# 304 of the 800 columns of a scatter of edges moved from five dense stages into two gather stages

## The chip, the cores and the metric

The kernel runs on one core of one Trainium2 chip. The metric is the device time of one launch in microseconds (us), a median over runs.

## The reference

A graph of 6250 nodes with 256 features and 100,000 edges (src, dst) goes through two layers. Cut to what matters here:

```
xn = layernorm(x)
# layer 0: two graph convolutions, each over all edges, then a linear attention and a linear layer
agg = segment_sum(relu(xn[src]), dst);   h = xn + agg;   out = relu(h @ w11 + b11) @ w12 + b12      # twice
x = x + relu(2 * out) + mix(xn);         x = x + layernorm(x) @ w.T + bias
# layer 1: attention over the same edges, but summed by src; a linear attention; a mixture of experts
e = exp(leaky_relu(el[src] + er[dst]));  w = e / segment_sum(e, src)[src];  out = segment_sum(w * x[dst], src)
```

Layer 0 sums by dst, the order in which the edges come. Layer 1 sums by src. So between the two the edges have to be put into the order of their sources.

## The kernel before

The program is a row of stages, each with its own semaphores and a barrier of all engines at its end; a stage ends with its slowest engine. Within one, every engine has its own instruction stream and they meet at semaphores. Nodes stand in 49 tiles of 128. The edges, packed into one int32 each (`m.packed`), stand as 125 lanes by 800 columns.

**Order by source.** `stage_count` counts the sources by tile. Inside the first convolution VectorE and TensorE then work out each edge's place: chunk c of 10 columns in round c (`Ranking.dve_read`, `dve_rank`, lines 789 to 796), 80 chunks, written over `m.key` as float32. At the end of that stage one VectorE cast makes `m.rank_i` of it (line 1058). After that the class `Scatter` (line 799 on) sends columns to DRAM (`m.edges[1]`): per column one indirect DMA on GpSimd's queue writes 125 single int32 values, each to its own place (line 818). It works in batches of 8: two small copies by GpSimd into staging tiles (lines 813, 814), a wait for them, 8 DMAs, and a wait for the batch two back. Five stages have it as GpSimd's only work, beside dense work on the other engines: mlp1 (144 columns), mlp2 (144), ffn (176), akv (176), aq (160). `stage_slots` reads the finished list before the attention over edges.

**A convolution** (`stage_conv`, conv1 and conv2) goes over 832 slots of 128 edges, 104 rounds of 8 (`RING`). GpSimd gathers 128 rows of 1 KB per slot (line 994), straight-line code without a loop; ahead of round r it waits until round r - 4 has been summed (its buffers) and until round r - 1 has landed:

```
for r in range(ROUNDS):
    if r >= DEEP: pool.wait_ge(summed, (r - DEEP + 1) * RING)
    if r >= 1:    pool.wait_ge(got[(r - 1) % DEEP], ...)      # round r - 1 has landed
    for k in range(RING): pool.indirect_dma_start(msg[...], None, table, ... m.GI[:, t:t + 1] ...)
```

ScalarE makes a one-hot of each slot's targets, TensorE multiplies it with the messages (line 1070), VectorE adds the product to the node's tile in `ACC` (line 1043). conv1 has the ranking beside it in rounds 0 to 79. conv2 has the keys' and values' sums of the linear attention beside it (`KeyValueSums`), with loads on SyncE's queue. The index lists of all gathers are the columns of `m.GI`, 896 wide.

After conv1 comes mlp1, then conv2, a short stage mix, mlp2, statistics, ffn, statistics, akv, aq, an addition, `stage_slots`, and the attention over edges.

Of the kernel before, what the change touches and what calls it, by code (L numbers as in the profile page):

```python
# [14 lines left out]
CH = 10  # L15
# [917 lines left out]

def stage_conv(nc, m, name, table, rank_sources, sum_keys):

# [1 line left out]
    with Stage(nc, name) as st:  # L941
# [5 lines left out]
        kv = KeyValueSums(nc, m, st) if sum_keys else None  # L947
        got = st.sems("got", DEEP)
        s_made, summed, added = st.sem("s_made"), st.sem("summed"), st.sem("added")
        tv, tt, ta = (st.sem(n) for n in ("turns_v", "turns_t", "turns_a"))  # L950
        ts = st.sem("turns_s")
        block = st.block()
        ROUNDS, CHUNKS = SLOT_TILES // RING, COLS // CH
# [23 lines left out]

        last_chunk = lambda r: isinstance(r, int) and r == CHUNKS - 1

        def landed(r, h):  # L980

            return (r - h) * (16 * RING // DEEP) + 16 * RING

        @block.gpsimd
        def _(pool):
            for r in range(ROUNDS):
                h = r % DEEP
                if r >= DEEP:
                    pool.wait_ge(summed, (r - DEEP + 1) * RING)
                if r >= 1:  # L990
                    pool.wait_ge(got[(r - 1) % DEEP], ((r - 1) // DEEP + 1) * 16 * RING)
                for k in range(RING):
                    t = r * RING + k
                    pool.indirect_dma_start(msg[:, h * RING + k, :], None, table,  # L994
                                            bass.IndirectOffsetOnAxis(ap=m.GI[:, t:t + 1], axis=0)).then_inc(got[h], 16)

        @block.scalar
        def _(act):
# [31 lines left out]
        def _(v):  # L1030
            def tile(r, h, chunk, keys):
                if chunk is not None:
                    ranking.dve_read(v, tv, r)
                    if not last_chunk(r):
                        ranking.dve_one_hot(v, tv, r + 1, 1 - h % 2)
                if keys is not None and h % 2 == 0 and not (isinstance(keys, int) and keys == 0):
                    kv.dve_norm(v, tv, keys - 1)
                starts = [v.snap(b * AW) for b in bins_of_round(nc, m, DVE, r)]
                for k in range(RING):
                    v.drain()  # L1040
                    v.wait_ge(summed, r * RING + k + 1)
                    acc = cols(m.ACC, starts[k], D)
                    nc.vector.tensor_tensor(acc, acc, ps[k % NB][:, 0:D], ALU.add).then_inc(added, 1)  # L1043
                if keys is not None and h % 2 == 1:
                    kv.dve_center(v, tv, keys)
                if chunk is not None:
                    ranking.dve_rank(v, r, h % 2)

            if sum_keys:
                nc.vector.memset(kv.vn[:, :, :], 1.0)  # L1050
# [3 lines left out]
            if sum_keys:  # L1054
                kv.dve_norm(v, tv, TILES - 1)
                kv.dve_end(v)
            if rank_sources:
                nc.vector.tensor_copy(m.rank_i[:, :], m.key[:, :])

        @block.tensor  # L1060
        def _(pe):
# [1381 lines left out]
def stages_before_attention(nc, m, dense):  # L2443
# [25 lines left out]
    stage_count(nc, m, 1)  # L2469
    stage_stats(nc, m, "stats0", 1e-5)  # L2470
    stage_norm(nc, m)
    stage_conv(nc, m, "conv1", m.relu_xn_table, True, False)

    stage_mlp(nc, m, "mlp1", m.w11s, m.b11s, m.w12s, m.b12r, False, (0, 144))
    stage_conv(nc, m, "conv2", m.conv1_table, False, True)
    m.wqkvs = sb("wqkvs", [P, 2, 3 * D])
    m.wouts = sb("wouts", [P, 2, D])
    m.boutr, m.mw2r = (sb(n, [P, D]) for n in ("boutr", "mw2r"))
    stage_mix(nc, m)
    stage_mlp(nc, m, "mlp2", m.w21s, m.b21s, m.w22s, m.b22r, True, (144, 144))  # L2480
    stage_stats(nc, m, "stats1", 1e-5)
    stage_ffn(nc, m, (288, 176))
    stage_stats(nc, m, "stats2", 1e-5, with_rms=True)
    stage_attn_kv(nc, m, (464, 176))
    stage_attn_q(nc, m, (640, 160))
    stage_attn_add(nc, m)
    stage_slots(nc, m, 1)

# [110 lines left out]
```

## Time and profile before

| | us |
|---|---|
| median of 3 runs (7104.03 to 7115.21) | 7106.12 |
| profiled execution, its own time | 7045.45 |
| its span, first to last instruction | 7043.1 |
| conv1: first gather to last addition | 358.6 to 1668.5 |
| mlp1 | 1669 to 1905 |
| conv2 | 1905 to 3215 |
| mlp2 | 3228 to 3466 |
| ffn | 3485 to 3772 |
| akv | 3794 to 4080 |
| aq | 4080 to 4343 |

Busy over the whole span: TensorE 49%, VectorE 40%, ScalarE 27%, GpSimd 51%. PE is TensorE's multiplications, PEld its loads of weights, DVE VectorE, ACT ScalarE, POOL GpSimd, SP SyncE. On GpSimd a DMA's duration is the time that the engine takes to issue it, not the transfer. A row of a timeline has start, duration, engine, line, operation, what is written and read, and in brackets the idle time before with what ended it; "issue" means that the trace names no releaser. A row of a table by stretches has the stretch, its length, then busy us with the count of instructions in brackets for PE, PEld, DVE, ACT and POOL, the granted clock of TensorE as a share of full speed, the mean busy share of the DMA engines and GB/s; where it is of one line, only that line's engine has a column.

### The profile page before, as it was taken

Reading aid. Unit: us, or ns where it says so; the run is one execution under the profiler, and the core shown is the slowest. Engines: PE = TensorE matmul, PEld = TensorE weight load, DVE = VectorE, ACT = ScalarE, POOL = GpSimd, SP = SyncE. Lnnn points to the kernel's source line nnn. Section 1 sums busy time; section 2 is a strip of 40 time slices with the busy share of each in tenths; the row PEclk is TensorE's granted clock in tenths of the full one; section 3 lists DMA queues with packets and bytes.
Section 4 is the critical chain, followed back from the end, with each engine's and each line's share of the span. In section 5 each row is a group of like instructions: output and inputs, shape, how many; then the busy total and the mean of one; then the engine's idle time right before and its main releaser. Section 6 shows DMA issues by size and latency. Waiting matters only on the chain. (4 is left out here: it accounts for less than half of the span.)

```text
span 7043.1 us, 79417 instructions
## 1 busy us (share of the span) xinstructions
PE 3443.0 (49%) x13479; PEld 2512.4 (36%) x13480; DVE 2838.6 (40%) x7047; ACT 1926.4 (27%) x4744; POOL 3563.8 (51%) x3729
## 2 busy tenths in 40 slices
PE   3445555445355555557423561244555552307990
PEld 0133333334244444446313451133434331204660
DVE  4644444422144444434422254444444446611222
ACT  0232222222233333332101210244444441112331
POOL 0066666666766666665676774455555551050005
PEclk9577777778777777778766786577777776558995
DMA  2232222223133333332101120011111111233113
GB/s 65 68 89 84 84 85 85 85 84 51 36 91 89 90 90 91 90 87 38 21 1 20 28 32 7 16 21 21 21 21 21 20 21 5 111 113 109 55 55 114
DMA packets 280599, 407.39 MB, mean 58 GB/s; under 512 B 93992, under 2 KB 197766, under 8 KB 280263
## 3 DMA queue, kind: packets, MB, share of 16 engines
q0 software_dynamic: 142720, 275.10, 16.6%
q1 hardware_dynamic: 137798, 131.50, 6.0%
q14 instruction: 65, 0.52, 0.0%
q8 instruction: 16, 0.26, 0.0%
HBM read 323.82 MB, written 81.61 MB: 58 GB/s over the span
## 5 line engine op out<-in xcount | busy, mean ns | idle before, releaser
L1070 PE MATMUL conv_ps<-conv_msg,conv_S 128*128 128x256 f32 x3328 | 1233.4, 549 | 1216.9 <-DMA conv_msg<-relu_xn_table,GI 659.2
L1070 PEld LDWEIGHTS conv_ps<-conv_msg,conv_S 128*128 128x128 f32 x3328 | 934.3, 290 | 1543.4 <-issue 1338.7
L1043 DVE TENSOR_TENSOR ACC<-ACC,conv_ps 128x256 f32 x1664 | 700.1, 421 | 1449.0 <-PE conv_ps L1070 1245.2
L994 POOL DMA_INDIRECT conv_msg<-relu_xn_table,GI x832 | 792.5, 953 | 702.7 <-DMA conv_msg<-relu_xn_table,GI 267.0
L1761 POOL DMA_INDIRECT gat_msg<-attn_table,GI x832 | 789.8, 949 | 602.9 <-DVE gat_M L1907 359.5
L994 POOL DMA_INDIRECT conv_msg<-conv_table,GI x832 | 786.8, 946 | 510.4 <-DMA conv_msg<-conv_table,GI 268.6
L1814 PE MATMUL gat_ps<-gat_M,gat_S 128*128 128x260 f32 x1664 | 645.1, 553 | 637.6 <-DVE gat_M L1907 601.6
L1014 ACT ACTIVATE conv_S<-iota_row,LOC 128x128 f32<-128x128 f32 x1664 | 507.9, 388 | 1019.0 <-PE conv_ps L1070 766.9
L1814 PEld LDWEIGHTS gat_ps<-gat_M,gat_S 128*128 128x128 f32 x1664 | 442.6, 281 | 748.6 <-issue 659.9
L1868 DVE TENSOR_TENSOR ACC<-ACC,gat_ps 128x260 f32 x832 | 351.9, 423 | 679.1 <-DMA conv_table<-mlp_a 427.7
L818 POOL DMA_INDIRECT edges_by_src<-mlp_lanes_pay,mlp_lanes_idx x288 | 342.7, 1190 | 109.7 <-issue 76.8
L2406 POOL DMA_INDIRECT combine_y<-expert_out,combine_at x98 | 97.1, 991 | 590.0 <-ACTq L2394 553.4
L1782 ACT COPY gat_ST<-gat_pst 128x1024 bf16<-128x1024 bf16 x104 | 105.2, 1012 | 740.3 <-DMA conv_msg<-relu_xn_table,GI 708.3
L1772 ACT ACTIVATE gat_SB<-iota_row,LOC 128x128 bf16<-128x128 f32 x832 | 254.4, 388 | 131.2 <-PEq L48 102.1
L1907 DVE TENSOR_TENSOR gat_M<-gat_msg,gat_M 128x512 f32<-128x512 f32 x416 | 284.1, 684 | 3.0 <-ACT gat_M L1798 2.9
L2369 DVE TENSOR_TENSOR experts_hb<-experts_ph,B1E 128x512 f32<-128x512 f32 x106 | 73.3, 691 | 447.9 <-PE experts_ph L2318 447.9
L1017 ACT ACTIVATE conv_S<-conv_S,ones 128x1024 f32<-128x1024 f32 x208 | 238.7, 1148 | 15.2
L818 POOL DMA_INDIRECT edges_by_src<-ffn_lanes_pay,ffn_lanes_idx x176 | 208.9, 1187 | 66.9 <-issue 46.9
L818 POOL DMA_INDIRECT edges_by_src<-akv_lanes_pay,akv_lanes_idx x176 | 208.0, 1182 | 67.0 <-issue 46.9
L2318 PE MATMUL experts_ph<-W1E,experts_xt 128*128 x424 | 213.0, 625 | 23.2 <-ACT experts_xt L2342 13.8
L818 POOL DMA_INDIRECT edges_by_src<-aq_lanes_pay,aq_lanes_idx x160 | 189.8, 1186 | 60.9 <-issue 42.6
L2298 PE MATMUL experts_po<-W2E,experts_ht 128*128 x848 | 200.4, 379 | 1.0 <-ACT experts_ht L2335 1.0
(388 smaller groups left out, 5171.4 us busy)
## 6 DMA issues: line engine op xcount, KB each, us to landing
expert_in<-router_zrow SPq DMA_DIRECT2D x53, 256.0 KB
experts_xe<-expert_in SPq DMA_DIRECT2D x106, 128.0 KB
expert_out<-experts_y SPq DMA_DIRECT2D x106, 128.0 KB
conv_msg<-relu_xn_table,GI POOLq DMA_INDIRECT x832
conv_msg<-conv_table,GI POOLq DMA_INDIRECT x832
gat_msg<-attn_table,GI POOLq DMA_INDIRECT x832
relu_xn_table<-norm_rx SPq DMA_DIRECT2D x49, 128.0 KB
xnT<-norm_xt SPq DMA_DIRECT2D x49, 128.0 KB
```

Source lines behind the costliest of these rows:

```text
L818: pool.indirect_dma_start(self.m.edges[self.which].rearrange("(e a) -> e a", a=1), bass.IndirectOffsetOnAxis(ap=self.idx[:, s, k:k + 1], a ...
L994: pool.indirect_dma_start(msg[:, h * RING + k, :], None, table, bass.IndirectOffsetOnAxis(ap=m.GI[:, t:t + 1], axis=0)).then_inc(got[h], 16)
L1014: nc.scalar.activation(S[:, h, k, :], m.iota_row[:, :], ACT.Square, bias=cols(m.LOC, r * RING + k, 1), scale=-1.0)
L1017: nc.scalar.activation(half, half, ACT.Relu, bias=m.ones[:, 0:1], scale=-1.0).then_inc(s_made, 1)
L1043: nc.vector.tensor_tensor(acc, acc, ps[k % NB][:, 0:D], ALU.add).then_inc(added, 1)
L1070: nc.tensor.matmul(ps[k % NB][:, 0:D], S[:, h % 2, k, :], msg[:, h * RING + k, :], start=True, stop=True).then_inc(summed, 1)
L1761: pool.indirect_dma_start(msg[:, h * RING + k, :], None, m.attn_table, bass.IndirectOffsetOnAxis(ap=m.GI[:, t:t + 1], axis=0)).then_inc(go ...
L1772: nc.scalar.activation(SB[:, h, k, :], m.iota_row[:, :], ACT.Square, bias=cols(m.LOC, r * RING + k, 1), scale=-1.0)
L1814: nc.tensor.matmul(bank, S[:, h % 2, k, :], M[:, h * RING + k, :], start=True, stop=True).then_inc(summed, 1)
L1868: nc.vector.tensor_tensor(acc, acc, bank_of(h, k), ALU.add).then_inc(added, 1)
L1907: last = nc.vector.tensor_tensor(Mg[:, :, 64 * q:64 * q + 64], msg[:, g1 * RING:(g1 + 1) * RING, 0:64], Mg[:, :, D + q:D + q + 1].broadcas ...
L2318: mm = nc.tensor.matmul(ph[s][:, :], xt[s][:, c * P:c * P + P], cols(m.W1E, e * (2 * HID) + c * HID, HID), start=(c == 0), stop=(c == 1))
```

## The change

`stage_conv` gets a range of columns. conv1 sends columns 0 to 95, one behind the gathers of each round from round 8 on; conv2 sends columns 96 to 303, two behind the gathers of every round. The DMA reads places and values straight from `m.rank_i` and `m.packed`, without staging. In conv1 it waits until the column's chunk has been ranked (`ranked`), and each chunk is now cast into `m.rank_i` right after its ranking, in place of the one cast at the stage's end. Behind the last round GpSimd waits for all of its scatters. The five dense stages send the other 496 columns: 112, 128, 48, 112 and 96. In all 800 as before.

```diff
--- before.py
+++ after.py
@@ -933,7 +933,7 @@
 
 
 
-def stage_conv(nc, m, name, table, rank_sources, sum_keys):
+def stage_conv(nc, m, name, table, rank_sources, sum_keys, columns):
 
 
 
@@ -947,6 +947,7 @@
         kv = KeyValueSums(nc, m, st) if sum_keys else None
         got = st.sems("got", DEEP)
         s_made, summed, added = st.sem("s_made"), st.sem("summed"), st.sem("added")
+        ranked, sent = st.sem("ranked"), st.sem("sent")
         tv, tt, ta = (st.sem(n) for n in ("turns_v", "turns_t", "turns_a"))
         ts = st.sem("turns_s")
         block = st.block()
@@ -977,6 +978,14 @@
 
         last_chunk = lambda r: isinstance(r, int) and r == CHUNKS - 1
 
+        def edge_columns(r):
+
+            first, count = columns
+            a_round = -(-count // ROUNDS)
+            lag = ROUNDS - count // a_round
+            j = (r - lag) * a_round
+            return range(first + j, first + j + a_round) if r >= lag else ()
+
         def landed(r, h):
 
             return (r - h) * (16 * RING // DEEP) + 16 * RING
@@ -993,6 +1002,13 @@
                     t = r * RING + k
                     pool.indirect_dma_start(msg[:, h * RING + k, :], None, table,
                                             bass.IndirectOffsetOnAxis(ap=m.GI[:, t:t + 1], axis=0)).then_inc(got[h], 16)
+                for j in edge_columns(r):
+                    if rank_sources:
+                        pool.wait_ge(ranked, j // CH + 1)
+                    pool.indirect_dma_start(m.edges[1].rearrange("(e a) -> e a", a=1),
+                                            bass.IndirectOffsetOnAxis(ap=m.rank_i[:, j:j + 1], axis=0),
+                                            m.packed[:, j:j + 1], None).then_inc(sent, 16)
+            pool.wait_ge(sent, 16 * columns[1])
 
         @block.scalar
         def _(act):
@@ -1045,6 +1061,7 @@
                     kv.dve_center(v, tv, keys)
                 if chunk is not None:
                     ranking.dve_rank(v, r, h % 2)
+                    nc.vector.tensor_copy(cols(m.rank_i, r * CH, CH), cols(m.key, r * CH, CH)).then_inc(ranked, 1)
 
             if sum_keys:
                 nc.vector.memset(kv.vn[:, :, :], 1.0)
@@ -1054,8 +1071,6 @@
             if sum_keys:
                 kv.dve_norm(v, tv, TILES - 1)
                 kv.dve_end(v)
-            if rank_sources:
-                nc.vector.tensor_copy(m.rank_i[:, :], m.key[:, :])
 
         @block.tensor
         def _(pe):
@@ -2469,20 +2484,20 @@
     stage_count(nc, m, 1)
     stage_stats(nc, m, "stats0", 1e-5)
     stage_norm(nc, m)
-    stage_conv(nc, m, "conv1", m.relu_xn_table, True, False)
-
-    stage_mlp(nc, m, "mlp1", m.w11s, m.b11s, m.w12s, m.b12r, False, (0, 144))
-    stage_conv(nc, m, "conv2", m.conv1_table, False, True)
+    stage_conv(nc, m, "conv1", m.relu_xn_table, True, False, (0, 96))
+
+    stage_mlp(nc, m, "mlp1", m.w11s, m.b11s, m.w12s, m.b12r, False, (304, 112))
+    stage_conv(nc, m, "conv2", m.conv1_table, False, True, (96, 208))
     m.wqkvs = sb("wqkvs", [P, 2, 3 * D])
     m.wouts = sb("wouts", [P, 2, D])
     m.boutr, m.mw2r = (sb(n, [P, D]) for n in ("boutr", "mw2r"))
     stage_mix(nc, m)
-    stage_mlp(nc, m, "mlp2", m.w21s, m.b21s, m.w22s, m.b22r, True, (144, 144))
+    stage_mlp(nc, m, "mlp2", m.w21s, m.b21s, m.w22s, m.b22r, True, (416, 128))
     stage_stats(nc, m, "stats1", 1e-5)
-    stage_ffn(nc, m, (288, 176))
+    stage_ffn(nc, m, (544, 48))
     stage_stats(nc, m, "stats2", 1e-5, with_rms=True)
-    stage_attn_kv(nc, m, (464, 176))
-    stage_attn_q(nc, m, (640, 160))
+    stage_attn_kv(nc, m, (592, 112))
+    stage_attn_q(nc, m, (704, 96))
     stage_attn_add(nc, m)
     stage_slots(nc, m, 1)
 
```

## Rows read from the trace of the kernel before

**Rows 1.** Busy time by stretches: two convolutions, then five stages' tails (columns told above).
```profile
358.60:1668.50 1309.90, 648.44 (x1825) 480.45 (x1825) 556.14 (x1152) 372.88 (x934) 792.49 (x832) 0.73 0.30 83
1905.00:3215.00 1310.00, 749.30 (x2162) 549.37 (x2162) 524.89 (x1374) 407.04 (x1034) 786.77 (x832) 0.73 0.32 88
1836.00:1905.00 69.00, 0.00 (x0) 0.00 (x0) 0.00 (x0) 0.00 (x0) 49.84 (x51) 0.50 0.08 3
3406.00:3465.70 59.70, 0.00 (x0) 0.00 (x0) 1.15 (x2) 0.00 (x0) 42.85 (x43) 0.50 0.07 1
3575.00:3772.00 197.00, 0.00 (x0) 0.00 (x0) 0.00 (x0) 0.00 (x0) 147.60 (x151) 0.50 0.07 1
3983.00:4079.70 96.70, 0.00 (x0) 0.00 (x0) 0.00 (x0) 0.00 (x0) 70.95 (x73) 0.50 0.07 1
4274.00:4342.80 68.80, 0.00 (x0) 0.00 (x0) 0.00 (x0) 0.00 (x0) 48.48 (x48) 0.52 0.07 1
```

**Rows 2.** Timeline of GpSimd across a change of round in conv1: start, duration, idle before.
```profile
713.94 0.95 POOL L994 DMA_INDIRECT conv_msg<-relu_xn_table,GI  x1 [0.30 <-issue]
717.47 0.94 POOL L994 DMA_INDIRECT conv_msg<-relu_xn_table,GI  x1 [2.58 <-DMA conv_msg<-relu_xn_table,GI]
```

**Rows 3.** Timeline of GpSimd in conv2: change of round, odd pause, wait near the end.
```profile
2518.87 0.95 POOL L994 DMA_INDIRECT conv_msg<-conv_table,GI  x1 [0.30 <-issue]
2522.39 0.94 POOL L994 DMA_INDIRECT conv_msg<-conv_table,GI  x1 [2.57 <-DMA conv_msg<-conv_table,GI]
2525.22 0.94 POOL L994 DMA_INDIRECT conv_msg<-conv_table,GI  x1 [1.88 <-issue]
...
3172.72 0.95 POOL L994 DMA_INDIRECT conv_msg<-conv_table,GI  x1 [6.56 <-DMA conv_msg<-conv_table,GI]
```

**Rows 4.** Who waited for whom, GpSimd in both convolutions: total, times, longest.
```profile
POOL conv_msg L994 <- DMA conv_msg<-conv_table,GI: 268.6, 102, 6.6
POOL conv_msg L994 <- DMA conv_msg<-relu_xn_table,GI: 267.0, 102, 6.3
```

**Rows 5.** Timeline of TensorE and VectorE at the start of a round of conv1.
```profile
902.81 5.84 PE L1070 MATMUL conv_ps<-conv_msg,conv_S 128*128 128x256 f32 x16 [6.51 <-DMA conv_msg<-relu_xn_table,GI]
904.15 0.42 DVE L1043 TENSOR_TENSOR ACC<-ACC,conv_ps 128x256 f32 x1 [3.75 <-PE conv_ps L1070]
```

**Rows 6.** Scatters of two tiles: duration shortest/median/longest in ns, first and last start.
```profile
L818 POOL DMA_INDIRECT edges_by_src<-mlp_lanes_pay,mlp_lanes_idx x288: 1172/1181/1456, 1670.6 to 3460.7; - x144
L818 POOL DMA_INDIRECT edges_by_src<-ffn_lanes_pay,ffn_lanes_idx x176: 1172/1181/1423, 3486.6 to 3767.3; - x176
```

**Rows 7.** Timeline across the end of ffn: last scatter, first work of the next stage.
```profile
3767.32 1.18 POOL L818 DMA_INDIRECT edges_by_src<-ffn_lanes_pay,ffn_lanes_idx  x1 [0.30 <-issue]
3772.70 1.40 DVE L301 BATCH_NORM_STATS2 stats_parts<-X  x4 [198.14 <-PEq L48]
```

**Rows 8.** Timeline of GpSimd in mlp1: the first scatters of two batches.
```profile
1876.67 1.19 POOL L818 DMA_INDIRECT edges_by_src<-mlp_lanes_pay,mlp_lanes_idx  x1 [0.91 <-POOL mlp_lanes_pay L814]
...
1889.50 1.19 POOL L818 DMA_INDIRECT edges_by_src<-mlp_lanes_pay,mlp_lanes_idx  x1 [0.92 <-POOL mlp_lanes_pay L814]
```

**Rows 9.** Timeline of VectorE and GpSimd across the end of conv1.
```profile
1667.92 0.57 DVE L1058 CAST rank_i<-key 125x800 int32<-125x800 f32 x1
1669.29 0.19 POOL L813 COPY mlp_lanes_idx<-rank_i 125x8 int32<-125x8 int32 x1 [13.97 <-POOLq L48]
```

**Rows 10.** Two VectorE lines: duration shortest/median/longest in ns, first and last start.
```profile
L666 DVE COPY base<-rank_below x20: 186/189/191, 125.0 to 253.1; 128x49 f32<-128x49 f32 x20
L1194 DVE TENSOR_SCALAR mlp_a<-mlp_b x49: 293/294/734, 1678.7 to 1834.8; 128x256 f32<-128x256 f32 x49
```

**Rows 11.** Scatters of mlp1 alone by stretch, dense work and tail: busy us (count).
```profile
1669.00:1836.00 167.00, 122.38 (x104) 0.97 0.19 39
1836.00:1905.00 69.00, 48.25 (x41) 0.50 0.08 3
```

**Rows 12.** Gathers of conv1: duration shortest/median/longest in ns, first and last start.
```profile
L994 POOL DMA_INDIRECT conv_msg<-relu_xn_table,GI x832: 940/946/1442, 358.6 to 1654.4; - x167
```

## The prediction

> **What bounds the kernel now.** I read the busy time by stretches first, then the GpSimd queue instruction by instruction inside the convolutions, then the ends of the stages that hold scatters. Two kinds of stretch bear on the change.
>
> In the five stages that scatter the edges (mlp1, mlp2, ffn, akv, aq) there is a tail in which TensorE and ScalarE do nothing, VectorE next to nothing, and GpSimd alone goes on: 69.0, 59.7, 197.0, 96.7 and 68.8 us, 491.2 us together [rows 1]. Each stage ends when its last scatter has landed.
>
> In the two convolutions (1310 us each) GpSimd is what sets the pace, though it is busy for 60% only [rows 1]. A round is 8 gathers at a pitch of 1.25 us; then GpSimd waits for the last of them to land before it issues the next round. The idle time there is 2.58 and 2.57 us in the rows shown [rows 2, 3]. Over a convolution such waits come to 267.0 and 268.6 us, 102 each [rows 4]. The second total holds the three waits at the end of 3.8, 6.56 and 6.1 us (the longest has its row [rows 3]); without them it is 252.1 / 99 = 2.55 us. TensorE waits for the same landing, 6.51 us before a round of 5.84 us, and VectorE is idle 3.75 us ahead of its first addition [rows 5]. So a convolution has 104 holes of about 2.55 us in GpSimd's own queue, 0.30 us of each being the gap that stands before every such DMA anyway.
>
> **The change part by part.** A scatter takes 1.181 us (1.172 to 1.456) plus the gap of 0.30 us [rows 6, 7], a pitch of 1.48 us.
>
> *Taken out of the five stages.* They go by batches of 8 columns: 12.83 us from batch to batch in the pair shown [rows 8], and over the whole ffn stage (3767.3 - 3486.6 - 7 x 1.48) / 21 = 12.87 us [rows 6]. I take 12.87.
> - mlp1, 144 to 112 columns: 4 batches, 51.5 us. Its tail is 69.0 us, so GpSimd still ends it and all of it counts.
> - mlp2, 144 to 128: 2 batches, 25.7 us, of a tail of 59.7. All of it counts.
> - ffn, 176 to 48: 16 batches, 205.9 us, more than the tail of 197.0. Dense work ends the stage now; the scatters are done some 9 us before. Saved 197.0.
> - akv, 176 to 112: 8 batches, 103.0 us, over a tail of 96.7. Saved 96.7, and the scatters are done 6 us before the dense work.
> - aq, 160 to 96: 8 batches, 103.0 us, over a tail of 68.8. Saved 68.8, with 34 us of cover.
>
> From the last dense instruction to the next stage it takes some 0.8 us (the cast ends at 1668.49, the next stage's first copy starts at 1669.29 [rows 9]), of which the tails' edges leave out some; I take 0.3 us off each of the last three. (With scatters last it was 5.4 us from the start of the last one to the next stage's work [rows 7]; that goes with the scatters and is in the tails.) The sum is 51.5 + 25.7 + 197.0 + 96.7 + 68.8 - 0.9 = 438.8 us saved. The cover is thin in akv: it is gone if each of its 112 scatters takes 0.06 us more, and from there costs 112 times the rest.
>
> *Put into conv1: 96 columns, one behind a round's gathers, from round 8 on.* From the end of the last gather: 0.30 + 1.18 + 0.30 = 1.78 us until the next gather could start, against the 2.58 us for which GpSimd waits anyway [rows 2]. Hidden, with 0.8 us of cover. All at the longest scatter of 1.456 us it is 2.06, still hidden. What is queued behind the scatter is the wait for the round's landing and the next 8 gathers; nobody notices while the landing is later. The new wait on the ranks is ahead of each scatter: column j needs chunk j // 10 and is sent in round j + 8, while VectorE ranks chunk c in round c, so it is always old.
>
> *Put into conv2: 208 columns, two behind each round.* 0.30 + 1.18 + 0.30 + 1.18 + 0.30 = 3.26 us against 2.55: 0.71 us too long. It applies at 100 of the 103 changes of round, as the three waits of 3.8 to 6.56 us at the end cover it: 71 us. GpSimd then no longer waits in conv2, and every round is 10.0 + 2.97 = 12.97 us. Nothing else is close: TensorE's round has 6.5 us of idle time in it. At the shortest price that I can argue, a gather's 0.94 us [rows 2] per scatter, the overrun is 0.23 us x 100 = 23 us; at the longest, 1.456, it is 1.26 x 100 = 126 us. I take 1.18, as that is the very instruction.
>
> *Small edits.* Once in 96 gathers, always at the same place of the straight-line program, GpSimd stands 1.88 instead of 0.30 us, for no releaser that the trace names: 8 times a convolution [rows 3]. If this goes with the length of the program (10 instructions of DMA or wait a round become 12), it is 1.6 more in each: 5 us in both, none if the landing covers them. The cast of all 800 ranks at the end of conv1, 0.57 us, goes [rows 9]; in its place come 80 casts of 10 columns inside the rounds, each about the 0.19 us of a copy of 128x49 [rows 10], on VectorE, which has 3.75 us to spare a round [rows 5]: nothing. The columns go out without the two staging copies and their waits of 1 us a batch; that is in the 12.87 removed. The last wait for all scatters stands behind the round whose gathers take 6 us to land: nothing.
>
> *The sum:* -438.8 + 71 + 5 - 0.6 = -363.4 us. The profiled execution took 7045.5 us, of which the span is 7043.1; it would be 6682. The median of the runs is 7106.1, 60.7 above the profiled one; I take that difference as it is, since what changes is inside the span: 6743 us, 5.1% faster.
>
> *The Trainium skill on a cost of the casts.* The rows first. In mlp1, while VectorE did two TENSOR_SCALAR from SBUF to SBUF a tile, 104 scatters took 122.38 us, 1.177 each; behind it, with VectorE idle, 41 took 48.25, again 1.177 [rows 11]. It was VectorE that was held: L1194 takes 0.294 us as a rule and up to 0.734 [rows 10]. SBUF - State Buffer, in the section on the two separate sides, says that a VectorE copy in a two-port mode locks GpSimd out of the port that it writes descriptors through, so that the DMA starves until the copy's end plus about 115 ns. That speaks against this change, which puts 80 such casts beside the gathers; the estimate by that page of the Trainium skill is 80 x (0.19 + 0.115) = 24 us more. The trace agrees that one waits for the other, but not that GpSimd is the one.
>
> **The rivals.**
> - *The casts hold GpSimd up.* 80 casts in conv1, all of them met by a gather: 80 x 0.19 = 15 us, or 80 x 0.44 (0.734 - 0.294) = 35 us. For it: a gather of conv1 took as much as 1.44 us where 0.946 is the median [rows 12]. Against it: the 1.177 twice [rows 11]. It gives 6758 to 6778. The page named above would have this one.
> - *A round's landing is put off by the scatters behind it, in part.* They share the queue, and the trace of before never has the two mixed. At half a scatter's pitch, 0.74 us each: conv1 +71 us; in conv2 the landing comes at 2.55 + 1.48 = 4.03 against 3.26, so the cost is 154 and not 71. -438.8 + 71 + 154 + 4 = -210: 6896 us. Against it: what is queued later has nothing to do with what landed earlier, and scatters alone pass at 1.48 us without a hold-up [rows 6, 7].
> - *The same in full: slower.* If a round counts as landed only once its scatters are through, each adds its whole 1.48 us: 304 x 1.48 = 450 us, and the time is 7106.1 - 438.8 + 450 + 4 = 7121, 0.2% slower. It decides from there: below 1.48 us a scatter the change wins. The same end is reached if a column read straight from the 800-wide tensor costs GpSimd 2.9 us in place of 1.18. The gathers read their indices in just that way from a tensor 896 wide and take 0.95 [rows 2].
> - *The change does not do what it says*, because the wait on the ranks holds the queue: excluded by the order of rounds above, but for a slip in the count; if it held GpSimd up long enough to eat the 363 us, the time would be 7106.
>
> DMA: Bandwidth & Descriptors, on queues, rings and completion order, says that a semaphore's increment lands only after every earlier write of its engine. By that page of the Trainium skill the scatters, which are later than their round's gathers, put nothing off there, and the next round's last gather comes 10 us behind them; no run so far shows it.
>
> **How the numbers follow.** The forecast, 6743, has 0.78, with 6720 to 6762 of its own; the casts 0.09; the landing put off in part 0.07; slower 0.03; no effect 0.01; the other 0.02 lie below, where a scatter in conv2 costs less than 1.18 (down to 6743 - 48 = 6695, at a gather's price). The range of 6710 to 6800 leaves all of these out, 0.13 together, and holds the forecast, the casts and the longest scatter (6743 + 55 = 6798). A measurement of this kernel tells 0.2%, 14 us, from no change. Faster by more than that: 0.96; within: 0.01; slower: 0.03.
>
> **What would show it.** Right: conv1 as long as before within 10 us, with 1.78 us of scatter inside holes that are still ended by the gathers' landing; conv2 longer by 70 to 80 us with pitch 12.97 and no more waits for landing; ffn, akv and aq ending with dense work and mlp1 and mlp2 with scatters. Wrong: holes after the scatters in conv1 longer than 0.9 us (landing put off), gathers well above the 792.49 / 832 = 0.953 us on the mean that they take in conv1 now [rows 1] (casts), or scatters above 1.2 us in the convolutions.

## The result, and the profile after

The kernel after takes 7192.52 us (median of 3, 7183.51 to 7215.11) against 7106.12: 1.0125 of before, 95% interval 1.0085 to 1.0164. It is slower by 86 us; 363 us less was forecast. Its profiled execution took 7215.11 us, with a span of 7213.4.

The busy time by stretches of after (columns as in [rows 1]): conv1, mlp1, conv2, mlp2, ffn, akv, aq, and the attention over edges, whose code the change doesn't touch.

```profile
357.80:1777.90 1420.10, 688.99 (x1825) 451.35 (x1825) 576.19 (x1232) 373.06 (x935) 917.01 (x928) 0.67 0.29 77
1777.90:1962.40 184.50, 118.90 (x686) 95.49 (x686) 51.37 (x147) 63.82 (x196) 137.86 (x140) 0.92 0.18 36
1963.00:3679.00 1716.00, 742.19 (x2162) 540.46 (x2162) 523.11 (x1374) 407.00 (x1034) 1041.40 (x1040) 0.68 0.26 68
3692.00:3901.00 209.00, 162.09 (x882) 137.03 (x882) 89.87 (x241) 63.94 (x196) 156.64 (x160) 0.93 0.22 35
3926.00:4018.00 92.00, 66.90 (x294) 43.85 (x294) 59.81 (x147) 18.23 (x49) 60.09 (x60) 0.97 0.06 1
4039.90:4242.00 202.10, 161.33 (x886) 135.89 (x886) 62.22 (x154) 70.13 (x246) 136.96 (x140) 0.95 0.20 41
4242.00:4448.00 206.00, 151.74 (x882) 134.78 (x882) 127.62 (x441) 37.32 (x98) 119.31 (x120) 0.88 0.18 32
4573.00:6011.00 1438.00, 671.69 (x3256) 518.00 (x3256) 620.47 (x1511) 597.01 (x1243) 785.23 (x832) 0.73 0.14 20
```

The whole stretches of before that answer to them, but for the convolutions, which stand in [rows 1]: mlp1, mlp2, ffn, akv, aq, attention over edges.

```profile
1668.50:1904.40 235.90, 112.94 (x686) 90.84 (x686) 50.61 (x147) 63.83 (x196) 176.86 (x180) 0.83 0.16 28
...
3228.00:3465.70 237.70, 154.65 (x882) 129.20 (x882) 93.49 (x247) 63.85 (x196) 178.63 (x180) 0.84 0.20 34
3485.00:3772.00 287.00, 66.74 (x294) 44.12 (x294) 59.48 (x147) 18.23 (x49) 216.14 (x220) 0.65 0.07 1
3793.80:4079.70 285.90, 162.41 (x886) 135.94 (x886) 62.09 (x154) 70.46 (x246) 215.01 (x220) 0.79 0.17 30
4079.70:4342.80 263.10, 140.22 (x882) 125.33 (x882) 128.12 (x441) 36.83 (x98) 196.42 (x200) 0.83 0.18 26
...
4463.00:5843.00 1380.00, 692.61 (x3256) 526.30 (x3256) 624.45 (x1511) 597.00 (x1243) 789.83 (x832) 0.73 0.14 21
```

The five dense stages gave what they should: 51 + 29 + 195 + 84 + 57 = 416 us less. conv1 took 110 us more and conv2 406 us more, where 0 and 71 stood in the sum. The 58 us of the untouched stage are no effect of the change: profiled again on one chip (e0_before, e0_after), before and after spent 1434 and 1432 us there. In that pair the account closes: 100 and 394 us more in conv1 and conv2, 427 less in the five dense stages, together 67 us, and the spans differ by 67 (7111.4 and 7178.3). The profiled execution of before that the rows come from was itself 61 us shorter than the median.

What happened in conv2 shows in three timelines. GpSimd across two changes of round, then VectorE and TensorE in the same stretch, then the row of GpSimd's waits for TensorE (total, times, longest, both convolutions):

```profile
2599.46 1.20 POOL L1008 DMA_INDIRECT edges_by_src<-packed,rank_i  x1 [0.30 <-issue]
2600.97 1.20 POOL L1008 DMA_INDIRECT edges_by_src<-packed,rank_i  x1 [0.30 <-issue]
2602.47 0.98 POOL L1003 DMA_INDIRECT conv_msg<-conv_table,GI  x1 [0.30 <-issue]
...
2614.03 1.20 POOL L1008 DMA_INDIRECT edges_by_src<-packed,rank_i  x1 [0.30 <-issue]
2623.31 0.98 POOL L1003 DMA_INDIRECT conv_msg<-conv_table,GI  x1 [8.08 <-PE conv_ps L1085]
```

```profile
2600.93 0.42 DVE L1059 TENSOR_TENSOR ACC<-ACC,conv_ps 128x256 f32 x1 [1.79 <-issue]
2618.02 0.42 DVE L1059 TENSOR_TENSOR ACC<-ACC,conv_ps 128x256 f32 x1 [16.67 <-DMA conv_table<-mlp_a]
```

```profile
2602.27 1.89 PE L1085 MATMUL conv_ps<-conv_msg,conv_S 128*128 128x256 f32 x8
2619.28 6.04 PE L1085 MATMUL conv_ps<-conv_msg,conv_S 128*128 128x256 f32 x16 [15.11 <-DVE ACC L1059]
```

```profile
POOL conv_msg L1003 <- PE conv_ps L1085: 474.8, 78, 8.2
```

The two scatters fill the place of the 2.57 us of [rows 3]: no gap is left at 2602.47. While GpSimd issues one DMA after another, until 2615.23, VectorE does no addition for 16.67 us. At the next change of round GpSimd itself stands for 8.08 us, since the sums that free its buffers aren't there; in that pause VectorE catches up. So rounds of 13.06 us (12.97 forecast) alternate with rounds of some 20.1 us. In conv1 one scatter leaves 0.8 us of the gap; 36 of its first 100 rounds take over 13.4 us, the longest 18.6 (in before 8, the longest 14.3).

The releaser named at 2618.02, a DMA of conv_table, had been done since mlp1. The trace shows what VectorE stood for: its sequencer had nothing more to do after 2606.53 and waited at the semaphore `summed`, which TensorE raises with each finished product. TensorE had issued four products between 2602.27 and 2604.16; the semaphore rises four times between 2617.89 and 2618.04, and VectorE goes on at 2617.91. Four products that were issued 0.43 us apart hardly end within 0.15 us, so it is the increments that come late, by some 14 us, and not the products. In conv2 of after this is no single case: 68 of 832 additions come over 2 us after the product was issued and VectorE had got to its wait, 575 us together, part of which falls into time that was idle anyway (conv1: 23 and 66 us). The trace lacks part of the semaphore's rises (it has 651 of 832 here), but 53 of the 68 waits end right behind a recorded one. In conv2 of before, and of e0_before, e0b_after, e3, e8 and c4 below, no wait of this sort is over 0.7 us.

### The profile page after: what moved, and what is told of

Its sections match the earlier page's. It is cut to its first block and busy times, and to the rows that moved or that the text cites. A ratio compares the mean times of both kernels' runs of the same rounds, so it can differ in the third digit from the quotient of the medians.

```text
span 7213.4 us, 79247 instructions
## 1 busy us (share of the span) xinstructions
PE 3479.3 (48%) x13479; PEld 2487.4 (34%) x13480; DVE 2853.4 (40%) x7126; ACT 1926.9 (27%) x4744; POOL 3566.2 (49%) x3653
## 5 line engine op out<-in xcount | busy, mean ns | idle before, releaser
L1085 PEld LDWEIGHTS conv_ps<-conv_msg,conv_S 128*128 128x128 f32 x3328 | 861.6, 272 | 2076.5 <-issue 1923.2
L1008 POOL DMA_INDIRECT edges_by_src<-packed,rank_i x304 | 367.0, 1207 | 92.7 <-issue 83.5
L818 POOL DMA_INDIRECT edges_by_src<-mlp_lanes_pay,mlp_lanes_idx x240 | 284.1, 1184 | 91.4 <-issue 64.0
L455 ACT ACTIVATE conv_sq<-conv_pkv 128x512 f32<-128x512 f32 x49 | 29.3, 597 | 705.2 <-DMA X<-in_x_dram 564.9
L2246 POOL DMA_INDIRECT expert_in<-dispatch_xm,dispatch_at x98 | 96.3, 983 | 201.8 <-DMA dispatch_xm<-xm 164.4
```

Of the source, the lines that this page charges most:

```text
L818: pool.indirect_dma_start(self.m.edges[self.which].rearrange("(e a) -> e a", a=1), bass.IndirectOffsetOnAxis(ap=self.idx[:, s, k:k + 1], a ...
L1008: pool.indirect_dma_start(m.edges[1].rearrange("(e a) -> e a", a=1), bass.IndirectOffsetOnAxis(ap=m.rank_i[:, j:j + 1], axis=0), m.packed[ ...
L1085: nc.tensor.matmul(ps[k % NB][:, 0:D], S[:, h % 2, k, :], msg[:, h * RING + k, :], start=True, stop=True).then_inc(summed, 1)
```

## The experiments

The texts put on record before the runs speak of five theories. A: GpSimd's idle gap lets the other engines get on, and filling it holds them up. A': it need not be idle, it must only pause in issuing indirect DMAs. B: the scatters' small writes disturb the others, wherever they stand. C: the slowness belongs to the conditions of the first measurement, and elsewhere the prediction's working holds. D: conv2 can't bear two scatters a round anywhere.

**Two kinds of chips.** The runs of this study fell on five chips, those of one batch always on one. On three of them (batches one, three and four) before took 6715 to 6725 us, on two (batches two and five) 7112 to 7113, like the 7106 of the result. I call these the 6720 kind and the 7110 kind; each ratio is against before on the same chip. Each chip was met in one batch only, so that the kind belongs to the chip, and not to the occasion, isn't shown.

| run | what it is | kind | us | ratio to before, 95% interval |
|---|---|---|---|---|
| e0_after | after | 7110 | 7170.8 | 1.0083 (1.0059 to 1.0107) |
| e0b_after | after | 6720 | 6321.7 | 0.9402 (0.9386 to 0.9417) |
| e0_before | before | 7110 | 7114.2 | 1.0000 (0.9990 to 1.0009) |
| e4_casts | before, casts in the rounds | 7110 | 7113.8 | 1.0002 (0.9992 to 1.0011) |
| e1, e1b | after, landing first | 6720 | 6606.1, 6607.8 | 0.9836, 0.9835 |
| e2 | one scatter a round | 6720 | 6420.6 | 0.9562 (0.9546 to 0.9578) |
| e5 | before, drain and fills | 6720 | 7095.9 | 1.0567 (1.0550 to 1.0585) |
| e3, e3b, e3c | before, no wait for landing | 6720 | 6240.7, 6237.9, 6246.2 | 0.9291, 0.9284, 0.9290 |
| e7 | after, no wait for landing | 7110 | 7246.3 | 1.0178 (1.0156 to 1.0199) |
| c3 | as e3, 48 columns moved | 7110 | 7249.4 | 1.0189 (1.0172 to 1.0206) |
| e8, e8b | before, paced by fills | 6720 | 6598.6, 6604.7 | 0.9822, 0.9822 |
| c4 | as e8, 48 columns moved | 7110 | 6935.9 | 0.9750 (0.9734 to 0.9766) |
| c2, c2b | e2, 64 columns beside aadd | 6720 | 6330.7, 6338.7 | 0.9422, 0.9426 |

**Before and after, on both kinds (e0_after, e0_before, e0b_after).** No edit.

> The kernel after, unchanged, again beside the kernel before. On the chip of the first runs here the kernel before takes 6715 us instead of 7106 us and one scatter a round left the rounds at 12.5 us. Theory C (what made after slow belongs to the conditions of the first measurement, where instructions of VectorE's and SyncE's sequencers took 0.7 us each; elsewhere the working of the prediction holds): -439 us in the dense stages, 0 in conv1, +71 us in conv2, +5 us: about 6350 us, ratio 0.946. Theory D (two scatters a round are what conv2 can't bear on any chip): conv2 alternates between 13 and 20 us a round, +400 us: about 6680 us, ratio 0.995 or more.

> The kernel before, unchanged, for its profile under the conditions of these runs. Theory C: no instructions of 0.7 us on VectorE's and SyncE's sequencers (18 and 109 of them in the first profile of before), rounds of 12.25 us in both convolutions as in the first profile, and the 300 us by which it is faster come from the stage that gathers behind the attention (1380 us then, about 1075 us here): 6715 us, ratio 1.000.

> The kernel after, unchanged, a second time, for the kind of chip it meets. Where before takes about 6715 us (no instruction of VectorE's or SyncE's sequencer takes 0.7 us there): theory C, the working of the prediction: -439 us in the dense stages and -25 us more since dense work is shorter there (150 us instead of 190 us, but GpSimd's columns end last in all but ffn, so nearly nothing of it counts), 0 in conv1, +71 us in conv2, +5: about 6350 us, ratio 0.946. Theory D (two scatters a round don't go through on any chip): 6680 us or more. Where before takes about 7110 us: 7170 us, ratio 1.008 again.

Theory C's number nearly came out on the 6720 kind, 6321.7 us for 6350; on the 7110 kind the loss came back, 1.0083. The numbers put down for e0_after and e0_before are for the 6720 kind, which that batch didn't meet; e0_before has the long instructions that its text expects to be gone. Stretches of conv1 and conv2 in e0b_after, and GpSimd across a change of round in each:

```profile
359.40:1674.00 1314.60, 648.67 (x1825) 480.89 (x1825) 570.43 (x1231) 372.89 (x934) 915.66 (x928) 0.73 0.31 83
...
1859.80:3244.00 1384.20, 750.87 (x2162) 550.81 (x2160) 525.15 (x1373) 406.34 (x1033) 1047.47 (x1040) 0.73 0.33 84
```

```profile
1003.33 1.21 POOL L1008 DMA_INDIRECT edges_by_src<-packed,rank_i  x1 [0.30 <-issue]
1005.57 0.98 POOL L1003 DMA_INDIRECT conv_msg<-relu_xn_table,GI  x1 [1.04 <-DMA conv_msg<-relu_xn_table,GI]
```

```profile
2617.91 1.21 POOL L1008 DMA_INDIRECT edges_by_src<-packed,rank_i  x1 [0.30 <-issue]
2619.42 1.20 POOL L1008 DMA_INDIRECT edges_by_src<-packed,rank_i  x1 [0.30 <-issue]
2620.92 0.98 POOL L1003 DMA_INDIRECT conv_msg<-conv_table,GI  x1 [0.30 <-issue]
```

Here conv1's scatter lies wholly inside the landing wait (0.30 + 1.21 + 1.04 = 2.55 us, the gap of [rows 2]), and conv2 takes 1384 us, 74 more than the 1310 of [rows 1], with 71 forecast. GpSimd's instructions take the same time on both kinds; it is the other engines that differ. Beside the late increments one thing shows it by itself: register instructions of VectorE's sequencer, then of SyncE's in akv, with their duration in ns (shortest/median/longest); in turn after, e0b_after, before, e0b_after.

```profile
L1057 DVEq ALU_OP  x1472: 1/40/1400, 415.3 to 3588.0; - x184
```

```profile
L1057 DVEq ALU_OP  x1472: 40/40/40, 417.1 to 3125.3; - x184
```

```profile
L1476 SPq FUSED_REGOPS  x46: 3/18/692, 3805.3 to 3973.5; - x46
```

```profile
L1491 SPq FUSED_REGOPS  x46: 46/46/51, 3610.1 to 3740.5; - x46
```

An instruction whose row names no tile and no wait takes 0.04 us each time on the 6720 kind, and up to 1.4 us on the 7110 kind, in stretches in which GpSimd issues indirect DMAs. Of the 1472 of this VectorE line, 173 are over 0.3 us in after, 6 in before and 17 in c4 below, which both pause, and none in e0b_after. The profile of before had it already in akv, where GpSimd sends batch after batch: 692 ns.

**The casts (e4).**

```
+ tensor_copy(cols(m.rank_i, r * CH, CH), cols(m.key, r * CH, CH))   # in round r, VectorE
- tensor_copy(m.rank_i[:, :], m.key[:, :])                           # end of conv1
```

> The kernel before with the 80 casts of a chunk's ranks in conv1's rounds, each behind its round's ranking, instead of one cast of all columns at the end; no scatters are moved. If the casts hold GpSimd or push VectorE's round (a rival of the prediction): conv1 longer by 15 to 40 us. If they cost nothing, as forecast: 6715 us, within 3 us of before.

1.0002 of before, on the 7110 kind (the 6715 us of its text are for the other). Eighty casts cost nothing; each took 0.173 us. The 24 us estimated by the Trainium skill, SBUF - State Buffer, on the two separate sides, are not there.

**Where the gap stays and the scatters come on top (e1, e1b), and one scatter a round (e2).**

```
+ if edge_columns(r): pool.wait_ge(got[h], (r // DEEP + 1) * 16 * RING)   # e1: ahead of the scatters
```

> The kernel after, with one wait added: GpSimd waits until its round's eight gathers have landed before it issues the scatters of that round, so that the gap in which it is idle stays as in the kernel before (about 2.5 us a round), and the scatters come on top. Theory A (the idle gap of GpSimd is what lets TensorE and VectorE get on; filling it starves them): rounds grow by the scatters alone, 96 x 1.5 us in conv1 and 104 x 3.0 us in conv2, and the alternation of 13 and 20 us in conv2 is gone: 7106 - 439 + 144 + 312 + 5 = about 7130 us, faster than after in spite of the added wait. Theory B (the scatters' 4-byte writes in themselves disturb the others, wherever they stand): the long rounds stay, and the wait comes on top: 7250 us or more.

> The kernel of e1 again (GpSimd waits for its round's landing before the scatters of that round). The runs so far were on two chips: on one the kernel before takes about 6715 us and nothing stalls, on the other about 7110 us and the kernel after loses. Where before takes about 7110 us: theory A (GpSimd's idle gap lets the others get on; filling it starves them): the long rounds are gone, rounds of 13.5 us in conv1 and 14.9 us in conv2 as on the other chip, 7113 - 439 + 96 x 1.4 + 104 x 2.5 + 60 (dense stages slower there, as in the profile of after) = about 7130 us, ratio 1.00, against 1.008 for after which lacks the wait. Theory B (the scatters' 4-byte writes disturb by themselves): the long rounds stay, 7250 us or more. Where before takes about 6715 us: 6606 us again.

> The kernel after, with one scatter a round in both convolutions (192 columns instead of 304; the dense stages take the other 608). If two scatters a round are what conv2 can't bear (they fill its gap), conv2 costs as conv1 did, about 90 to 110 us instead of 400, and the dense stages save 439 x 192/304 = 277 us: 7106 - 277 + 200 = about 7030 us, faster than both kernels. If the number of scatters counts in proportion (1.7 us each as in conv2 and conv1 of the profile together): 7106 - 277 + 327 = about 7155 us.

Both fell on the 6720 kind alone, where nothing stalls in any kernel, so they do not tell A from B. They price the place: with the gap kept empty, 96 scatters on top made conv1 1417 us long; with the same 96 inside it (e2) it took 1313, and conv2 1314. So a scatter on top costs 104 / 96 = 1.1 us there and one inside nothing. Neither kernel was timed on the 7110 kind.

**Fills in the gap (e5).**

```
+ for k in range(1 if rank_sources else 3): pool.drain(); nc.gpsimd.memset(filler[:, :], 0)
```

> The kernel before, with work of GpSimd that moves nothing over DMA behind each round's gathers: one fill of 128x1024 bytes in a round of conv1 and three in a round of conv2 (an estimate of 1.0 and 3.1 us from the row of the 128x520 fill, 0.54 us). Theory A in its plain form (any busy GpSimd starves the others): about as the kernel after's convolutions, +90 to +110 us in conv1 and +400 us in conv2, so about 7600 us. Theory A' (only an unbroken stream of indirect DMAs does it) and theory B (the scatters' writes): conv1 unchanged, conv2 longer by what sticks out of the 2.55 us gap, 0.6 us x 104: about 7170 us.

```profile
715.20 0.95 POOL L995 DMA_INDIRECT conv_msg<-relu_xn_table,GI  x1 [0.30 <-issue]
718.72 0.95 POOL L999 MEMSET conv_filler<- 128x1024 uint8 x1 [2.57 <-issue]
719.82 0.95 POOL L995 DMA_INDIRECT conv_msg<-relu_xn_table,GI  x1
```

The timeline shows why this run can't answer its question: the drain ahead of the fill waited 2.57 us, as long as the wait for the landing in before [rows 2], and the fill came behind the gap and not into it. It also met the 6720 kind, where the question doesn't arise. e8 below does without the drain.

**No gap at all, with scatters and without (e3, e3b, e3c, e7, c3).**

```
- if r >= 1: pool.wait_ge(got[(r - 1) % DEEP], ((r - 1) // DEEP + 1) * 16 * RING)
```

e3 takes this line out of before, e7 out of after; c3 is e3 with the last 48 columns of aq sent during the addition (aadd).

> The kernel before, without any scatter in the convolutions, and without GpSimd's wait for the landing of the round before: it waits for the tiles of four rounds ago alone. Theory A (without an idle gap the others starve): the rounds do not fall to the ten us that eight gathers take; they stay at 12 to 13 us with long ones of 16 to 20 us between, as in the kernel after: 7100 to 7300 us. Theory B (the scatters themselves disturb): rounds fall to about 10.5 us, 208 x 1.8 us less: about 6730 us.

> The kernel of e3 again (before without GpSimd's wait for the landing, no scatters in the convolutions), which took 0.929 of before where before takes 6715 us. Where before takes about 7110 us: theory A: an unbroken run of gathers stalls the others with no scatter in it; rounds of 10 us alternate with rounds of 14 to 18 us, 12.5 to 14 us in the mean: 7110 to 7400 us, ratio 1.00 to 1.04. Theory B (the scatters are what stalls): rounds near 10 us, ratio 0.93 to 0.95. Where before takes about 6715 us: 6241 us again.

> Before without GpSimd's wait for the landing and without scatters in the convolutions; 0.929 of before twice where before takes 6715 us. Where before takes about 7110 us: theory A (an unbroken run of indirect DMAs, of whatever kind, holds up the other engines' sequencers there): rounds of 10 us alternate with long ones, ratio 1.00 to 1.04, and several hundred 0.7 us instructions on VectorE's sequencer. Theory B (it takes the scatters' writes): rounds near 10 us, ratio 0.93 to 0.95, few such instructions.

> The kernel after without GpSimd's wait for the landing of the round before. Without that wait the convolutions' rounds are GpSimd's own work: 10.0 us (as measured in the kernel before without the wait), and each scatter adds its 1.5 us: 11.5 us in conv1, 13.0 us in conv2. If the scatters cost what they cost GpSimd and nothing more: 6241 - 439 + 96 x 1.5 + 208 x 1.5 + 5 = about 6265 us, no better than the kernel before without the wait: once the gap is gone there is nothing left to hide a scatter in. If the writes disturb the rounds: more than 6350 us.

> Before without GpSimd's wait for the landing in the convolutions, no scatters there, and 48 of the columns moved from the attention's query stage into the stage that adds the attention. Where before takes about 6720 us: 6241 - 48 x 1.6 = about 6165 us, ratio 0.918, the fastest of all here. Where before takes about 7110 us: theory A (an unbroken run of gathers holds up the others): long rounds with no scatter in the convolutions at all, ratio 0.99 to 1.03; theory B: 0.93.

On the 6720 kind the rounds fall to 10.0 us and the kernel to 0.929 of before. On the 7110 kind the same convolutions are longer than with the wait. e7's 6265 us were worked out for the 6720 kind; on the 7110 kind it took 7246.3. The stretches of conv1 and conv2, first of e3 on the 6720 kind, then of c3 on the 7110 kind:

```profile
359.20:1435.00 1075.80, 609.89 (x1819) 449.53 (x1820) 554.63 (x1148) 372.92 (x935) 805.15 (x832) 0.80 0.37 102
1674.00:2751.00 1077.00, 682.27 (x2166) 485.45 (x2166) 533.62 (x1390) 407.10 (x1034) 789.42 (x832) 0.81 0.39 107
```

```profile
358.90:1725.00 1366.10, 624.62 (x1824) 431.86 (x1825) 558.20 (x1149) 373.02 (x934) 791.28 (x832) 0.70 0.29 80
1963.00:3432.00 1469.00, 751.26 (x2166) 547.91 (x2166) 527.80 (x1390) 407.45 (x1036) 786.40 (x832) 0.71 0.29 79
```

There isn't one scatter in c3's convolutions. GpSimd and VectorE in its first rounds:

```profile
408.03 0.94 POOL L992 DMA_INDIRECT conv_msg<-relu_xn_table,GI  x1 [0.30 <-issue]
415.44 0.94 POOL L992 DMA_INDIRECT conv_msg<-relu_xn_table,GI  x1 [6.47 <-PE conv_ps L1068]
```

```profile
396.28 0.42 DVE L1041 TENSOR_TENSOR ACC<-ACC,conv_ps 128x256 f32 x1 [4.36 <-remote]
...
406.77 0.42 DVE L1041 TENSOR_TENSOR ACC<-ACC,conv_ps 128x256 f32 x1 [5.17 <-remote]
411.69 0.42 DVE L1041 TENSOR_TENSOR ACC<-ACC,conv_ps 128x256 f32 x1 [4.49 <-remote]
415.19 0.42 DVE L1041 TENSOR_TENSOR ACC<-ACC,conv_ps 128x256 f32 x1 [3.08 <-PE conv_ps L1068]
415.81 0.42 DVE L1041 TENSOR_TENSOR ACC<-ACC,conv_ps 128x256 f32 x1 [0.20 <-issue]
...
425.32 0.42 DVE L1041 TENSOR_TENSOR ACC<-ACC,conv_ps 128x256 f32 x1 [0.20 <-issue]
```

Late in GpSimd's unbroken row of gathers, VectorE does one addition in 5 us. GpSimd's last gather ends at 408.97, and 6.2 us behind it the additions come every 0.62 us. They are as quick after GpSimd has begun again at 415.44; only from 431.21 on are they slow once more (1.92, 3.15 and 3.10 us idle before three of them). So the delay doesn't set in at once: here it comes some 15 us after a pause, in conv2 of after some 10 us (the pause ended at 2589.41, the first slow addition is that of 2600.93). That is why short and long rounds alternate. In e7 the first long round likewise comes in rounds that have no scatter yet (the scatters begin in round 8):

```profile
408.45 0.95 POOL L1001 DMA_INDIRECT conv_msg<-relu_xn_table,GI  x1 [0.30 <-issue]
415.92 0.94 POOL L1001 DMA_INDIRECT conv_msg<-relu_xn_table,GI  x1 [6.52 <-PE conv_ps L1083]
```

Theory B, that the scatters' small writes disturb, falls for these rounds: gathers alone do it. Theory A stands. That after's own rounds are long by this and nothing else is argued from the likeness (rounds of 13 and 20 us, the same late increments: 56 in conv2 of c3, 347 us); no run on this kind had the scatters with the gap kept.

**A gap in which GpSimd works but issues no DMA (e8, e8b, c4).** Before, without the wait for the landing, and behind each round's gathers:

```
+ for k in range(2):
+     if r + k: pool.wait_ge(filled, r * 2 + k)        # its own fill before: long done
+     nc.gpsimd.memset(filler[:, :], 0).then_inc(filled, 1)
```

> The kernel before with GpSimd's wait for the landing replaced by work of its own that issues no DMA: two fills of 128x1024 bytes behind each round's gathers (0.95 us each in e5's profile, about 2.1 us with what lies between them). No scatters. Where before takes about 7110 us: theory A in the form that GpSimd must be idle for the others to get on: as without the wait, long rounds, ratio 1.00 to 1.04. Theory A' (what starves the others is an unbroken stream of indirect DMAs being issued, not a busy GpSimd): rounds of 12.1 us, no long ones, ratio 0.995 to 1.00. Where before takes about 6715 us: rounds of 12.1 us under both, ratio 0.99 to 1.00.

> Before with the wait for the landing replaced by two fills behind the gathers (1.83 us a round in which GpSimd works and issues no DMA; rounds of 11.85 us and ratio 0.982 where before takes 6715 us). Where before takes about 7110 us: theory A' (a gap in the issuing of DMAs is enough, GpSimd may work in it): rounds of 11.85 us with few long ones, ratio 0.98 to 0.99. Theory A (GpSimd must be idle): long rounds, ratio 1.00 or more.

> The paced kernel (the wait for the landing replaced by two fills, 1.83 us a round without a DMA issued) with the same 48 columns moved. Where before takes about 6720 us: 6600 - 77 = about 6525 us, ratio 0.971. Where before takes about 7110 us: theory A' (a gap in the issuing of DMAs is enough): rounds of 11.85 us, few long ones, 7113 - 85 - 50 = about 6980 us, ratio 0.981; theory A (GpSimd must be idle): long rounds, ratio 1.00 or more.

c4 fell on the 7110 kind. GpSimd across a change of round, and the stretches of conv1 and conv2:

```profile
2399.93 0.95 POOL L993 DMA_INDIRECT conv_msg<-conv_table,GI  x1 [0.30 <-issue]
2400.88 1.98 POOL L998 MEMSET conv_filler<- 128x1024 uint8 x2
2403.01 0.95 POOL L993 DMA_INDIRECT conv_msg<-conv_table,GI  x1 [0.16 <-issue]
```

```profile
358.70:1617.00 1258.30, 656.25 (x1821) 489.03 (x1822) 555.63 (x1149) 372.95 (x935) 1002.32 (x1040) 0.72 0.31 87
1857.00:3116.00 1259.00, 741.04 (x2166) 541.63 (x2165) 565.80 (x1389) 406.71 (x1033) 989.65 (x1040) 0.75 0.33 92
```

No round of conv2 is over 12.0 us and none of conv1 over 12.4, though GpSimd is hardly ever idle. 2.13 us a round without a DMA being issued are enough, and neither the landing wait nor an idle GpSimd is needed: theory A'. c4 is also the fastest version timed on that kind, 0.975 of before (0.981 forecast): 55 and 52 us less in the convolutions (1313.3 and 1310.8 in e0_before), 54 in aq, the rest in small pieces. On the 6720 kind, without the moved columns (e8, e8b), the rounds are 11.84 us and the kernel 0.9822 of before. Whether it is the length of the pause that counts, or how closely the DMAs stand on the whole, no run tells apart: 8 DMAs in 11.9 us go well (c4), 9 in 12.3 us (the short rounds in conv1 of after) don't.

**A version for the other kind (c2, c2b).** e2 with 64 columns sent beside the addition of the attention, and (192, 112), (304, 128), (432, 64), (496, 128), (624, 112) in the dense stages:

```
+ @block.gpsimd
+ def _(pool): scatter.columns(pool, *columns)      # stage_attn_add, (736, 64)
```

> A version meant to beat both: one scatter a round in both convolutions (96 + 96 columns), 64 columns in the stage that adds the attention, where GpSimd has nothing to do, and 544 in the five dense stages (112, 128, 64, 128, 112). Where before takes about 6715 us: e2 measured 6421 us for 192 + 608 columns; 64 columns fewer in its dense stages (-25 -26 -25 -0 -25 us at 1.6 us a column where GpSimd ends last) and +8 us in the adding stage: about 6330 us, ratio 0.943. Where before takes about 7110 us: dense and adding stages 195 + 207 + 105 + 205 + 200 + 105 = 1017 us against 1406 us, less 389 us; each convolution +100 us as conv1 of after, which has the same one scatter a round: about 6925 us, ratio 0.973.

> The version of c2 again (one scatter a round, 64 columns beside the adding of the attention), which took 0.942 of before where before takes 6715 us. Where before takes about 7110 us: 389 us less in the dense and adding stages, +100 us in each convolution as conv1 of after: about 6925 us, ratio 0.973; if one scatter a round costs conv2 much more than conv1 (its VectorE does more), up to 7000 us, ratio 0.985.

6330.7 us for 6330 forecast, 6338.7 the second time: on this kind costs add up by GpSimd's own prices. It only draws level with after itself (0.9402); the best there is e3, 0.929. On the 7110 kind it has no run.

## Why the prediction was wrong, step by step

- *Taken out of the five stages, 438.8 us:* right within 23 us. On the 7110 kind 416 us, since akv and aq end with dense work now, as forecast, but took 202.1 and 206.0 us and not 285.9 - 96.7 = 189.2 and 263.1 - 68.8 = 194.3. On the 6720 kind mlp1 to aq saved more, aq 101 us instead of 68.8 (262.4 us with 160 columns in e8, 161.2 in e0b_after): dense work is done sooner there and the tail was longer. Thus even there the kernel did not gain the 363 us forecast but 403.5 (6725.2 to 6321.7).
- *conv1, hidden in the landing wait:* **the step that failed.** "Hidden, with 0.8 us of cover" took the 2.58 us of [rows 2] for idle time that belongs to nobody. On the 7110 kind it is the time in which the increments and the sequencers of the others catch up. Filling 1.78 of it cost 110 us, 1.1 us a scatter; on the 6720 kind the step was right (1314.6 us, against 1309.9 in [rows 1] and 1313.3 in e0_before).
- *conv2, 71 us:* the pitch was right (13.06 against 12.97) and the sentence behind it wrong: "nothing else is close: TensorE's round has 6.5 us of idle time in it" [rows 5]. That idle time was there, but only behind a gap in GpSimd's issuing; the increments of TensorE that VectorE waits for came late without it. conv2 took 406 us more, 335 above the sum, the larger part of the miss; on the 6720 kind 74.
- *Casts, last wait, landing not put off:* right (e4; the gap of 2.55 us with a scatter in it, which is also what the Trainium skill, DMA: Bandwidth & Descriptors, on completion order, led one to expect: the trace agrees). Of the rivals none was this one. "The landing put off in full" ended at 7121 us, near the result, by another mechanism. (Its second way there doesn't come out by the prediction's own sum: scatters of 2.9 us would give some 7175 us, and 7121 is reached at 2.7.)
- *The range*, 6710 to 6800, went by prices of GpSimd's own instructions alone. It had no case in which another engine slows down because GpSimd doesn't pause, though three places of before spoke of it: the register instructions of 692 ns in akv; the wait for the landing, which the order of the data doesn't need (e3 does without it); and the attention over edges, the one stage that gathers without such a wait. There GpSimd stood for VectorE, and VectorE had itself been idle just before (before; GpSimd, then VectorE):

```profile
5021.36 0.94 POOL L1761 DMA_INDIRECT gat_msg<-attn_table,GI  x1 [3.31 <-DVE gat_M L1907]
```

```profile
5017.01 0.43 DVE L1868 TENSOR_TENSOR ACC<-ACC,gat_ps 128x260 f32 x1 [3.70 <-DMA conv_table<-mlp_a]
```

What stays open: why two kinds of chips differ in this, and what GpSimd's issuing shares with the semaphore increments and register instructions of other engines that makes these late. No run shows either. How short the gap may be lies between 0.8 us (conv1 of after: long rounds) and 2.13 (c4: none). That the gap kept empty would also save after itself on the 7110 kind wasn't tried.

## What to carry to other kernels

An idle gap of the engine that sets the pace isn't free until one knows what the others do in it: before filling it, look in the trace for stages where the gap is missing, for short instructions of the other sequencers that are long there, and for an engine that stands though what it waits for was issued long before. Where GpSimd issues indirect DMAs in a long row, leave some 2 us a round without one, or put GpSimd's compute work there. And time a change of a few per cent on more than one chip: this one is 6% faster on a chip of one kind and 1% slower on one of the other.

## What the runs showed of the hardware

- An unbroken run of indirect DMAs on GpSimd stretched register instructions of VectorE's and SyncE's sequencers from 0.04 to up to 1.4 us on some chips and not at all on others (40/40/40 ns). On the same chips TensorE's increments of a semaphore reached VectorE late: in conv2 of after it stood up to 12.1 us at its wait for a product already issued, in before 0.7. The attention over edges, which gathers without such a pause, with the same code took 1434 us on the 7110 kind (e0_before) and 1076 on the 6720 kind (e3b).
- A drain on GpSimd behind eight gathers waited 2.57 us, as long as their landing takes (e5).
- An indirect write of 125 single int32 values takes GpSimd 1.20 us and a pitch of 1.50, read straight from an 800-wide tensor; a gather of 128 rows of 1 KB 0.95 and 1.25.
